# A two-layer graph kernel: all sixteen first-layer tiles split, whole-tile high halves in two buffers, the bias added by an accumulating DMA

## The chip, the cores and the metric

The kernel runs on one core of a Trainium2 chip. The metric is the device time of one execution in microseconds (us). The kernel before takes 984.5 us in the median of three runs.

## The reference

Eight graphs (B = 8) of N = 2048 nodes with F = 128 features. Layer 0 is an attention layer over a dense matrix `adj`, layer 1 a graph convolution with batch normalisation over all eight graphs:

```python
# layer 0, one graph
h = x @ W
e = h @ a1 + (h @ a2).T                 # [N, N]
e = where(e >= 0, e, 0.2 * e)
attention = softmax(adj * e, axis=0)    # over the rows i
x = attention @ h + bias + x
# layer 1, one graph
y = adj @ (x @ W1 + b1)
# over all graphs and nodes
y = relu((y - mean(y)) * rsqrt(var(y) + 1e-5) * gamma + beta)
out = y + x
```

## The kernel before

Everything is held transposed: features (or source nodes j) on the 128 partitions, the 2048 nodes i along the row. A graph is a batch (`bt`, numbered 0 to 7, `par` = its parity) and is worked off in 16 tiles of 128 source nodes, each a 128x2048 block (1 MB) of `adjT`, held in one of 18 slots. Four chunks of 512 columns make up a row; PSUM has four banks `acc0` for layer 0 and four banks `acc1` for layer 1.

Layer 0, one tile t: ScalarE makes the edge scores from the row vector f1 and a column of f2 (`edge`, L533); VectorE multiplies by the adjacency and finds the maximum of each partition (`score`, L656); ScalarE negates it (L540) and takes the exponential with its sum (`exp`, L542); VectorE takes the reciprocal (`recip`, L663); GpSimd scales the 128x128 block of h with it (`scale_h`, L793); TensorE multiplies into `acc0`. In batch 0 and in tiles 0, 4, 8 and 12 of the later batches ("whole" tiles) this is one float32 matmul for each chunk (`layer0`, L406), which the trace shows as two records. In the other twelve tiles of batches 1 to 7 (`SPLIT`) both operands are split into a rounded high half (type fp32r) and a rest: ScalarE writes the high half of the exponentials chunk by chunk into four 2 KB buffers `exp_hi` (`exp_high`, L552), VectorE the rest in place (`exp_low`, L675), GpSimd the halves of hz (L802, L805), and TensorE makes three one-record matmuls for each chunk (`layer0_split`, L420 to L422). `scores` is a ring of four tiles: `edge` of tile t waits until TensorE is done with tile t-4.

Layer 1 of batch b-1 runs on TensorE between the layer-0 tiles of batch b: `layer1` (L441), float32, one tile of it ahead of each layer-0 tile. It is three tiles ahead, so its last one stands ahead of tile 13, and tiles 13, 14 and 15 of layer 0 follow each other directly. `SIGMA` is the order in which layer 1 takes the slots, and so in which they are loaded again.

At the end of a batch come, for each chunk, h of the next batch (`make_h`, L390, out of an x that was loaded to a slot) and the layer-1 input of this batch (`make_support`, L428), which needs `make_xp` on VectorE (L701: attention sum plus residual and bias). ScalarE copies y of the layer just finished from PSUM (L583) and h (L578), VectorE takes statistics of y (L695) and adds b1 (`support_from_psum`, L707). Layer 1 of the batch can start when h is out of `acc1` and the first chunk of the support is ready. GpSimd adds the bias to the residual x (`add_bias`, L811), the bias having been loaded by SyncE into the f1 buffer of that parity, which is free when the last `edge` of the batch is done. There are two f1 buffers.

All transfers are issued by SyncE, in program order: where one waits, all behind it wait. Batch 0 also multiplies the x of all other batches with a1 and a2 (`rows_of_f`, L375). The last layer 1 (batch 7) is split too (L455 to L458).

Of the kernel before, what the change touches and what calls it, by code (L numbers as in the profile page):

```python
# [27 lines left out]
F32 = mybir.dt.float32  # L28
F32R = mybir.dt.float32r
# [5 lines left out]
P = 128  # L35
# [19 lines left out]
def build(nc, adjT, xT, biasT, W, WT, a12, W1, b1, gamma, beta, outT):  # L55
# [8 lines left out]
    ER = 4  # L64

    SPLIT = [t for t in range(NT) if t % 4]

    LAST_SPLIT = list(range(1, NT))
    WHOLE = [t for t in range(NT) if t not in SPLIT]
    NS = NC * len(SPLIT)  # L70


    SIGMA = list(range(PRE, NT - 2)) + [1, NT - 2, NT - 1, 0]
    assert NT % ER == 0 and len(SPLIT) % 2 == 0 and NT - 1 in SPLIT and 0 in WHOLE
# [6 lines left out]
    X_STAGE = {0: slot_of(1, 0), 1: slot_of(1, 1), **{b: NT - B + b for b in range(2, B)}}  # L81
    STAGED = set(X_STAGE[b] for b in range(1, B))

# [4 lines left out]
    with ExitStack() as ctx:  # L88
# [21 lines left out]
        f1_odd, sup_lo = sb_two_types("f1_odd", "sup_lo", [P, N])  # L110
        f1_all = [sb("f1_even", [P, N]), f1_odd]
        region = [sb("region_even", [P, N]), sb("region_odd", [P, N])]
        exp_hi = [sb(f"exp_hi{c}", [P, CH], F32R) for c in range(NC)]
# [17 lines left out]

        wt_sb = scores[ER - 1][:, 0:P]
# [5 lines left out]
        f_sb = f1_all[1][0:NF, :]  # L138
# [7 lines left out]
        bias_loaded = [sem(f"bias_loaded{c}") for c in range(NC)]  # L146
        gb_loaded = sem("gb_loaded")
        f2_loaded = sem("f2_loaded")
        f_stored, f1_loaded = sem("f_stored"), [sem("f1_loaded_even"), sem("f1_loaded_odd")]
        x0_loaded = [sem(f"x0_loaded{c}") for c in range(NC)]  # L150
        x_loaded = [sem(f"x_loaded{c}") for c in range(NC)]
# [6 lines left out]
        whole_used = sem("whole_used")  # L158
        split_used = sem("split_used")
# [16 lines left out]
        ident_set, hz_done, xb_done = sem("ident_set"), sem("hz_done"), sem("xb_done")  # L176
# [7 lines left out]
        def adj_value(bt, t):  # L184

            if t == 0:
                return 16 * (bt.half + 1)
            if t < PRE:
                return 16 * (bt.n + 1)
            return 16 * (bt.n + 1 + (t in STAGED))  # L190

        def chunk_count(bt, t, c):


            return NS * bt.n + NC * SPLIT.index(t) + c + 1

        def wait_l0(eng, bt, t):

            if t in SPLIT:
                eng.wait_ge(split_used, chunk_count(bt, t, NC - 1))  # L200
            else:
                eng.wait_ge(whole_used, len(WHOLE) * bt.n + WHOLE.index(t) + 1)

# [38 lines left out]
        for b in range(2, B):  # L242
            earlier[slot_of(b % 2, 1)] += 1
# [7 lines left out]
        def _(sp):  # L251
# [11 lines left out]

            def load_f1(bt):
                if not (isinstance(bt.n, int) and bt.n < 2):
                    sp.wait_ge(xb_done, NC * (bt.n - 1))
                sp.dma_start(f1_all[bt.par][:, :], f_rows[bt.n - 1].partition_broadcast(P)).then_inc(f1_loaded[bt.par], 16)

            def load_bias(bt):
                sp.wait_ge(edge_out, NT * (bt.n + 1))  # L270
                for c in range(NC):
                    sp.dma_start(f1_all[bt.par][:, cols(c)], biasT[:, cols(c)]).then_inc(bias_loaded[c], 16)
# [6 lines left out]
            def step(bt):  # L279
                nx = bt.next()  # L280
                if is_first(bt):
                    for t in range(1, NT):
                        for b in F_STEP:
                            if max(F_STEP[b], 1) == t:
                                load_x(b, X_STAGE[b])
# [9 lines left out]
                    load_f1(nx)  # L295
                    sp.wait_ge(h_mm, NC)
                    load_adj(nx, 0)
                    for c in range(NC - 1):
                        load_residual(bt, c)
                    load_bias(bt)  # L300
                    load_residual(bt, NC - 1)
                else:
                    pv = bt.prev()
                    for k, t in enumerate(SIGMA):
# [3 lines left out]
                        elif not is_last(bt):  # L308
                            if t == 1:
# [551 lines left out]
```

## Time and profile before

| | us |
|---|---|
| median of three runs (981.13 to 985.25) | 984.5 |
| the profiled execution | 981.78 |
| its span, first to last instruction | 980.0 |
| TensorE busy | 914.9 (93%) |
| ScalarE busy | 802.3 (82%) |
| VectorE busy | 696.0 (71%) |
| GpSimd busy | 439.8 (45%) |

Busy is the time in which an engine has an instruction under way. "Idle before, releaser" is the time an engine stood still ahead of an instruction and what ended it. In a timeline each row has the start, the duration, the engine, the source line, what is written and read, and in square brackets the idle time ahead of it. The records of matmuls overlap a little, so the pitch from one start to the next tells what one costs, not the duration. The granted TensorE clock is 0.986 of full speed over the span.

### The profile page before, as it was taken

How to read it: one execution, taken by the hardware profiler on the slowest of the kernel's cores; microseconds unless marked ns; L12 is line 12 of the kernel's file. 1: busy time of each engine (PE TensorE's matmuls, PEld its weight loads, DVE VectorE, ACT ScalarE, POOL GpSimd, SP SyncE). 2: the span in 40 equal slices, each digit the busy share in tenths (PEclk: the TensorE clock that was granted, in tenths of full speed). 3: DMA queues.
4: the chain of work that ended last, by engine and by line, in shares of the span. 5: the costliest groups of instructions: out<-in, count | busy, mean ns of one | idle time of the engine just before them, and what ended most of it. 6: DMA issues, size and time to landing. Idle time of an engine off the chain costs nothing.

```text
span 980.0 us, 9394 instructions
## 1 busy us (share of the span) xinstructions
PE 914.9 (93%) x3055; PEld 528.9 (54%) x3055; DVE 696.0 (71%) x864; ACT 802.3 (82%) x953; POOL 439.8 (45%) x334
## 2 busy tenths in 40 slices
PE   7998999989999899999999899998999999998970
PEld 4333555555555655556555555556555555555760
DVE  2544477777777867777777967778777777779967
ACT  6877599986999789996999779996999969896746
POOL 1544355562555435562555635553555625554000
PEclk9999999999999999999999999999999999999995
DMA  8956454566456664566456664475546555435968
GB/s 321 422 227 223 158 197 169 215 227 215 176 183 233 212 220 167 214 221 225 172 183 225 225 219 156 168 265 202 204 182 225 190 218 204 168 128 193 385 253 342
DMA packets 45132, 213.91 MB, mean 218 GB/s; under 512 B 5406, under 2 KB 6030, under 8 KB 23438
## 3 DMA queue, kind: packets, MB, share of 16 engines
q1 hardware_dynamic: 45084, 213.32, 59.7%
q8 instruction: 24, 0.39, 0.2%
q14 instruction: 24, 0.20, 0.1%
HBM read 189.07 MB, written 24.23 MB: 218 GB/s over the span
## 4 chain that ended last, share of the span: by engine, by line
PE 79%; DVE 6%; issue 6%; POOL 4%; ACT 3%; DMA 0%; DVEq 0%; SPq 0%; ACTq 0%; POOLq 0%
PE acc L441 40%; PE acc L406 11%; PE acc L421 6%; PE acc L422 6%; PE acc L420 6%; POOL hz L793 3%; PE acc L428 3%; DVE exp_lo L675 3%; PE acc L390 2%; DVE stats L695 2%; PE acc L455 1%; PE acc L457 1%; PE acc L458 1%; ACT scores L542 1%; DVE adj_slot L781 1%
## 5 line engine op out<-in xcount | busy, mean ns | idle before, releaser
L656 DVE CUSTOM_DVE_ANT_0 scores<-scores,adj_slot 128x2048 f32<-128x2048 f32 x128 | 294.0, 2297 | 24.0 <-DMA adj_slot<-adjT 21.4
L675 DVE TENSOR_TENSOR exp_lo<-scores,exp_hi 128x512 fp32r<-128x512 f32 x336 | 268.5, 849 | 35.5 <-ACT exp_hi L552 35.4
L542 ACT ACTIVATE scores<-scores,neg_mx 128x2048 f32<-128x2048 f32 x128 | 256.3, 2002 | 4.2
L793 POOL TENSOR_TENSOR hz<-region_even,rz 128x128 f32<-128x128 f32 x64 | 132.6, 2072 | 222.1 <-DVE rz L663 222.1
L441 PE MATMUL acc<-adj_slot,region_even 128*128 128x512 f32 x512 | 228.8, 592 | 0.0
L552 ACT CAST exp_hi<-scores 128x512 fp32r<-128x512 f32 x336 | 190.6, 615 | 41.0 <-PE acc L422 37.5
L793 POOL TENSOR_TENSOR hz<-region_odd,rz 128x128 f32<-128x128 f32 x64 | 124.2, 1940 | 215.4 <-DVE rz L663 215.4
L420 PE MATMUL acc<-exp_hi,hz_lo 128*128 128x512 f32 x336 | 162.1, 482 | 15.6 <-DVE exp_lo L675 8.7
L441 PE MATMUL acc<-adj_slot,region_odd 128*128 128x512 f32 x392 | 175.2, 592 | 0.0
L406 PE MATMUL acc<-scores,hz 128*128 128x512 f32 x352 | 158.7, 595 | 6.2 <-POOL hz L793 5.0
L441 PEld LDWEIGHTS acc<-adj_slot,region_even 128*128 128x128 f32 x512 | 96.7, 190 | 106.2 <-issue 103.4
L663 DVE RECIPROCAL rz<-zsum 128x1 f32<-128x1 f32 x128 | 20.9, 164 | 184.3 <-ACT scores L542 184.3
L533 ACT ACTIVATE scores<-f_even,f_cols 128x2048 f32<-128x2048 f32 x64 | 127.5, 1993 | 8.2 <-PE acc L406 7.3
L421 PE MATMUL acc<-exp_hi,hz_hi 128*128 128x512 f32 x336 | 131.4, 391 | 0.0
L422 PE MATMUL acc<-exp_lo,hz_hi 128*128 128x512 f32 x336 | 131.2, 390 | 0.0
L533 ACT ACTIVATE scores<-f_odd,f_cols 128x2048 f32<-128x2048 f32 x64 | 127.4, 1993 | 0.5 <-issue 0.5
L441 PEld LDWEIGHTS acc<-adj_slot,region_odd 128*128 128x128 f32 x392 | 74.0, 190 | 81.1 <-issue 79.0
L406 PEld LDWEIGHTS acc<-scores,hz 128*128 128x128 f32 x352 | 65.9, 190 | 94.4 <-issue 93.5
L420 PEld LDWEIGHTS acc<-exp_hi,hz_lo 128*128 128x128 f32 x336 | 63.2, 188 | 53.7 <-issue 21.4
L421 PEld LDWEIGHTS acc<-exp_hi,hz_hi 128*128 128x128 f32 x336 | 63.2, 188 | 26.3 <-issue 16.7
L422 PEld LDWEIGHTS acc<-exp_lo,hz_hi 128*128 128x128 f32 x336 | 63.1, 188 | 13.6
L805 POOL TENSOR_TENSOR hz_lo<-hz,hz_hi 128x128 fp32r<-128x128 f32 x84 | 62.3, 742 | 6.6
(75 smaller groups left out, 676.5 us busy)
## 6 DMA issues: line engine op xcount, KB each, us to landing
adj_slot<-adjT SPq DMA_DIRECT2D x128, 1024.0 KB, 4.8
adj_slot<-xT SPq DMA_DIRECT2D x13, 1024.0 KB, 9.6
adj_slot<-xp_dram SPq DMA_DIRECT2D x8, 1024.0 KB, 6.3
adj_slot<-y_dram SPq DMA_DIRECT2D x7, 1024.0 KB, 6.6
outT<-adj_slot SPq DMA_DIRECT2D x6, 1024.0 KB, 4.7
f_odd<-f_rows SPq DMA_DIRECT2D x4, 1024.0 KB, 6.9
region_even<-xT SPq DMA_DIRECT2D x16, 256.0 KB, 5.5
f_even<-biasT SPq DMA_DIRECT2D x16, 256.0 KB, 6.8
```

Of the source, the lines that this page charges most:

```text
L406: mm = pe.matmul(acc0[c][:, :], hz[e][:, :], scores[e][:, cols(c)], start=(t == 0), stop=(t == NT - 1))
L420: pe.matmul(acc0[c][:, :], hz_lo[e][:, :], exp_hi[c][:, :], start=False, stop=False)
L421: pe.matmul(acc0[c][:, :], hz_hi[m % 2][:, :], exp_hi[c][:, :], start=False, stop=False)
L422: pe.matmul(acc0[c][:, :], hz_hi[m % 2][:, :], exp_lo[e][:, cols(c)], start=False, stop=(t == NT - 1)).then_inc(split_used, 1)
L441: mm = pe.matmul(acc1[c][:, :], region[bt.par][:, tile_cols(t)], slots[slot_of(bt.par, t)][:, cols(c)], start=(k == 0), stop=(k == NT - 1))
L533: act.activation(scores[t % ER][:, :], f1_all[bt.par][:, :], ACT.Prelu, bias=f2_cols[:, bt.n, t:t + 1], alpha=ALPHA).then_inc(edge_out, 1)
L542: act.activation(scores[e][:, :], scores[e][:, :], ACT.Exp, bias=neg_mx[:, e:e + 1], accum_out=zsum[:, e:e + 1]).then_inc(exp_done, 1)
L552: act.copy(exp_hi[c][:, :], scores[e][:, cols(c)]).then_inc(hi_done, 1)
L656: dve.tensor_tensor_reduce(scores[e][:, :], scores[e][:, :], slots[s][:, :], 1.0, NEG_BIG, ALU.mult, ALU.max, mx[:, e:e + 1]).then_inc(max ...
L675: dve.tensor_tensor(exp_lo[e][:, cols(c)], scores[e][:, cols(c)], exp_hi[c][:, :].bitcast(F32), ALU.subtract).then_inc(lo_done, 1)
L793: scaled = pool.tensor_tensor(hz[e][:, :], region[bt.par][:, tile_cols(t)], rz[:, e:e + 1].to_broadcast([P, P]), ALU.mult)
L805: pool.tensor_tensor(hz_lo[e][:, :], hz[e][:, :], hz_hi[m % 2][:, :].bitcast(F32), ALU.subtract).then_inc(hz_done, 1)
```

## The change

All 16 tiles of batches 1 to 7 take the split path. The high halves get two buffers of a whole tile (`hi`, 8 KB a partition each) in place of four chunk buffers: one cast and one subtraction for a tile, except tile 15, which has four parts (`PARTS`). `exp_high` of tile t waits for TensorE's end of tile t-2 (`HR` = 2) and now stands ahead of `edge` of tile t+2. The negation of the maximum goes from ScalarE to VectorE, and the copy of y from PSUM too, where it stands with its statistics ahead of the last `exp_low`. `edge`, `exp` and `exp_high` of the next batch's tile 0 stand ahead of the copies of h; on VectorE, `score` of that tile stands ahead of `make_xp`, and its `exp_low` ahead of `support_from_psum`. There is one f1 buffer, loaded again when all edges of a batch are done. The x for `make_h` is loaded by chunks into the region of the next batch once y has been stored from there. The bias is added to the residual by a DMA from GpSimd's queue that accumulates into SBUF.

```diff
-    SPLIT = [t for t in range(NT) if t % 4]
+    HR = 2
+    PARTS = {t: (NC if t == NT - 1 else 1) for t in range(NT)}
-    SIGMA = list(range(PRE, NT - 2)) + [1, NT - 2, NT - 1, 0]
+    SIGMA = list(range(PRE, NT)) + list(range(PRE))
-        exp_hi = [sb(f"exp_hi{c}", [P, CH], F32R) for c in range(NC)]
+        hi_x, hi = zip(*[sb_two_types(f"hi_x{e}", f"hi{e}", [P, N]) for e in range(HR)])
...
+            def load_x_for_h(bt, c):
+                sp.wait_ge(y_stored[c], 16 * (bt.n - 1))
+                sp.wait_ge(stats_done, NC * (bt.n - 2) + c + 1)
+                sp.dma_start(region[bt.par][:, cols(c)], xT[bt.n][:, cols(c)]).then_inc(xh_loaded[c], 16)
             def load_f1(bt):
-                if not (isinstance(bt.n, int) and bt.n < 2):
-                    sp.wait_ge(xb_done, NC * (bt.n - 1))
+                sp.wait_ge(edge_out, NT * bt.n)
...
                         if k == 14:
                             load_residual(bt, 2)
-                        if k == 14:
-                            load_bias(bt)
-                    load_residual(bt, 3)
+                        if k == 14 and not is_last(bt):
+                            load_f1(nx)
                     for c in range(NC):
                         sp.wait_ge(y_out, NC * pv.n + c + 1)
                         sp.dma_start(y_dram[pv.n][:, cols(c)], region[pv.par][:, cols(c)]).then_inc(y_stored[c], 16)
+                    load_residual(bt, 3)
+                    if not is_last(bt):
+                        for c in range(NC):
+                            load_x_for_h(nx, c)
+                        load_adj(nx, 1)
                 store_xp(bt)
...
             def exp(bt, t):
-                act.wait_ge(max_done, NT * bt.n + t + 1)
-                act.mul(neg_mx[:, e:e + 1], mx[:, e:e + 1], -1.0).then_inc(neg_done, 1)
             def exp_high(bt, t):
-                for c in range(NC):
-                    act.wait_ge(split_used, NS * bt.n + NC * (m - 1) + c + 1)
-                    act.copy(exp_hi[c][:, :], scores[e][:, cols(c)]).then_inc(hi_done, 1)
+                if t >= HR:
+                    wait_l0(act, bt, t - HR)
+                elif bt.n == 1:
+                    act.wait_ge(h_mm, NC * 2)
+                else:
+                    wait_l0(act, bt.prev(), t - HR + NT)
+                for i in range(PARTS[t]):
+                    act.copy(hi[m][:, part_cols(t, i)], scores[e][:, part_cols(t, i)]).then_inc(hi_done, 1)
...
             def add_bias(bt, c):
                 pool.wait_ge(x_loaded[c], 16 * (bt.n + 1))
-                pool.wait_ge(bias_loaded[c], 16 * (bt.n + 1))
-                pool.tensor_tensor(region[bt.par][:, cols(c)], region[bt.par][:, cols(c)],
-                                   f1_all[bt.par][:, cols(c)], ALU.add).then_inc(xb_done, 1)
+                pool.dma_start(region[bt.par][:, cols(c)], biasT[:, cols(c)], accum_op=ALU.add).then_inc(xb_done[c], 16)
```

VectorE's queue at the end of batch 1, before: `exp_lo3` is tile 15, `acc0` into `region_odd` is `make_xp`, `adj_slot0` is the score of the next batch's tile 0.

```order
L663 RECIPROCAL rz<-zsum 128x1 [waits hz_done,exp_done]
L675 TENSOR_TENSOR exp_lo3_70<-scores3,exp_hi0 128x512 [waits hi_done]
...
L695 BN_STATS stats<-region_even 128x6 [waits y_out] x4
L701 TENSOR_TENSOR region_odd<-acc0_0,region_odd 128x512 [waits xb_done,split_used]
...
L701 TENSOR_TENSOR region_odd<-acc0_3,region_odd 128x512 [waits xb_done,split_used]
L656 ISA scores0,mx<-scores0,adj_slot0 128x2048 [waits edge_out,slot_loaded0]
...
L707 TENSOR_TENSOR region_odd<-acc0_0,b1_sb 128x512 [waits xp_stored0,sup_mm]
```

The same place with the change; `acc1` into `region_even` is the copy of y, `exp_lo0` the rest of the next batch's tile 0.

```order
L660 RECIPROCAL rz<-zsum 128x1 [waits hz_done,exp_done]
L692 COPY region_even<-acc1_0 128x512 [waits l1_chunk]
...
L697 BN_STATS stats<-region_even 128x6 [waits y_out] x4
L672 TENSOR_TENSOR exp_lo3_70<-scores3,hi1_73 128x512 [waits hi_done] x4
L651 ISA scores0,mx<-scores0,adj_slot0 128x2048 [waits edge_out,slot_loaded0]
L651 ISA mx 128x1
L654 TENSOR_SCALAR neg_mx<-mx 128x1 [waits max_done]
L703 TENSOR_TENSOR region_odd<-acc0_0,region_odd 128x512 [waits xb_done0,l0_chunk]
...
L703 TENSOR_TENSOR region_odd<-acc0_3,region_odd 128x512 [waits xb_done3,l0_chunk]
L660 RECIPROCAL rz<-zsum 128x1 [waits hz_done,exp_done]
L672 TENSOR_TENSOR exp_lo0_67<-scores0,hi0_72 128x2048 [waits hi_done]
L709 TENSOR_TENSOR region_odd<-acc0_0,b1_sb 128x512 [waits xp_stored0,sup_mm]
```

Copies and statistics of y moved ahead of the last rests, the next score ahead of `make_xp`, and the rest of the next tile 0 between `make_xp` and the support.

ScalarE's queue at the same batch end, before: `scores3` is tile 15, then y, the edge of the next tile 1, and h.

```order
L542 ACTIVATE scores3,zsum<-scores3,neg_mx 128x2048 [waits neg_done]
L552 CAST exp_hi0<-scores3 128x512 [waits split_used,exp_done]
...
L583 COPY region_even<-acc1_0 128x512 [waits l1_chunk]
...
L533 ACTIVATE scores1<-f1_even,f2_cols 128x2048 [waits split_used]
L578 COPY region_even<-acc1_0 128x512 [waits stats_done,y_stored0,h_mm]
```

And with the change; `scores0` and `scores1` are tiles 0 and 1 of the next batch.

```order
L543 ACTIVATE scores3,zsum<-scores3,neg_mx 128x2048 [waits neg_done]
L557 CAST hi1_73<-scores3 128x512 [waits l0_tile,exp_done]
L557 CAST hi1_73<-scores3 128x512 x3
L536 ACTIVATE scores0<-f1_all,f2_cols 128x2048 [waits l0_tile,f1_loaded]
L536 ACTIVATE scores1<-f1_all,f2_cols 128x2048 [waits l0_tile]
L543 ACTIVATE scores0,zsum<-scores0,neg_mx 128x2048 [waits neg_done]
L557 CAST hi0_72<-scores0 128x2048 [waits l0_tile,exp_done]
L580 COPY region_even<-acc1_0 128x512 [waits h_mm]
```

The copies of y have left this queue, and two edges, an exponential and a whole cast now stand ahead of the copies of h.

## Rows read from the trace of the kernel before

**Rows 1.** Stretch of one batch: us, busy time (instructions) of PE, PEld, DVE, ACT, POOL; clock; DMA

```profile
227.30:340.70 113.40, 109.98 (x370) 64.38 (x369) 84.68 (x108) 96.86 (x121) 56.97 (x44) 1.00 0.57 204
```

**Rows 2.** Timeline of PE, batch 3: start, duration, line, operation, records

```profile
401.60 3.60 PE L406 MATMUL acc<-scores,hz 128*128 128x512 f32 x8
405.03 3.60 PE L441 MATMUL acc<-adj_slot,region_even 128*128 128x512 f32 x8
...
411.20 3.59 PE L441 MATMUL acc<-adj_slot,region_even 128*128 128x512 f32 x8
```

**Rows 3.** Timeline of PE at that batch's end and the next one's start

```profile
430.40 3.60 PE L441 MATMUL acc<-adj_slot,region_even 128*128 128x512 f32 x8
...
441.57 0.50 PE L420 MATMUL acc<-exp_hi,hz_lo 128*128 128x512 f32 x1 [0.64 <-POOL hz_lo L805]
...
445.33 1.05 PE L390 MATMUL acc<-w_sb,adj_slot 128*128 128x128 f32 x8
447.40 1.16 PE L428 MATMUL acc<-w_sb,region_odd 128*128 128x128 f32 x8 [1.02 <-DVE region_odd L701]
...
453.76 7.03 PE L441 MATMUL acc<-adj_slot,region_odd 128*128 128x512 f32 x16
```

**Rows 4.** Groups by line: count, total us, mean ns, idle before

```profile
L675 DVE TENSOR_TENSOR exp_lo<-scores,exp_hi 128x512 fp32r<-128x512 f32 x336 | 268.5, 849 | 35.5 <-ACT exp_hi L552 35.4
L542 ACT ACTIVATE scores<-scores,neg_mx 128x2048 f32<-128x2048 f32 x128 | 256.3, 2002 | 4.2
L533 ACT ACTIVATE scores<-f_odd,f_cols 128x2048 f32<-128x2048 f32 x64 | 127.4, 1993 | 0.5 <-issue 0.5
L683 DVE TENSOR_TENSOR adj_lo<-adj_slot,exp_lo 128x2048 fp32r<-128x2048 f32 x15 | 33.8, 2288 | 3.0 <-ACT exp_lo L562 3.0
L562 ACT CAST exp_lo<-adj_slot 128x2048 fp32r<-128x2048 f32 x15 | 28.5, 1917 | 9.2 <-PE acc L458 9.2
```

**Rows 5.** Timeline of DVE at the same batch end

```profile
440.30 4.07 DVE L675 TENSOR_TENSOR exp_lo<-scores,exp_hi 128x512 fp32r<-128x512 f32 x4 [0.48 <-ACT exp_hi L552]
444.30 2.46 DVE L695 BATCH_NORM_STATS2 stats<-region_even 128x6 f32<-128x512 f32 x4
446.68 2.46 DVE L701 TENSOR_TENSOR region_odd<-acc,region_odd 128x512 f32<-128x512 f32 x4
449.06 2.28 DVE L656 CUSTOM_DVE_ANT_0 scores<-scores,adj_slot 128x2048 f32<-128x2048 f32 x1
```

**Rows 6.** Timeline of SP's queue and of POOL: a residual chunk issued, and its bias added

```profile
441.55 0.33 SPq L262 DMA_DIRECT2D region_odd<-xT  x1
...
445.00 1.28 POOL L811 TENSOR_TENSOR region_odd<-region_odd,f_odd 128x512 f32<-128x512 f32 x1 [1.78 <-DMA region_odd<-xT]
```

**Rows 7.** DMA issues: KB of each, median us from issue to landing

```profile
f_odd<-f_rows SPq DMA_DIRECT2D x4, 1024.0 KB, 6.9
region_even<-xT SPq DMA_DIRECT2D x16, 256.0 KB, 5.5
f_even<-biasT SPq DMA_DIRECT2D x16, 256.0 KB, 6.8
...
y_dram<-region_even SPq DMA_DIRECT2D x16, 256.0 KB, 3.8
```

**Rows 8.** Timeline of POOL in batch 0: the scaling of tiles 14 and 15

```profile
97.27 2.50 POOL L793 TENSOR_TENSOR hz<-region_even,rz 128x128 f32<-128x128 f32 x1 [2.39 <-DVE rz L663]
102.16 0.40 POOL L793 TENSOR_TENSOR hz<-region_even,rz 128x128 f32<-128x128 f32 x1 [2.39 <-DVE rz L663]
```

**Rows 9.** Timeline of PE in batch 0 and at its end

```profile
23.04 3.67 PE L406 MATMUL acc<-scores,hz 128*128 128x512 f32 x8 [1.10 <-issue]
28.16 3.67 PE L406 MATMUL acc<-scores,hz 128*128 128x512 f32 x8 [1.45 <-POOL hz L793]
...
78.00 10.93 PE L406 MATMUL acc<-scores,hz 128*128 128x512 f32 x24
...
106.86 1.05 PE L390 MATMUL acc<-w_sb,adj_slot 128*128 128x128 f32 x8
```

More of the change, by code:

```diff
@@ L64, in build @@
     ER = 4
-    SPLIT = [t for t in range(NT) if t % 4]
+    HR = 2
+    PARTS = {t: (NC if t == NT - 1 else 1) for t in range(NT)}
+    NL = sum(PARTS.values())
     LAST_SPLIT = list(range(1, NT))
-    WHOLE = [t for t in range(NT) if t not in SPLIT]
-    NS = NC * len(SPLIT)
-    SIGMA = list(range(PRE, NT - 2)) + [1, NT - 2, NT - 1, 0]
-    assert NT % ER == 0 and len(SPLIT) % 2 == 0 and NT - 1 in SPLIT and 0 in WHOLE
+    SIGMA = list(range(PRE, NT)) + list(range(PRE))
+    assert NT % ER == 0 and NT % HR == 0
     assert F == P and B == 8 and NT == 16 and sorted(SIGMA) == list(range(NT))
@@ L175, in build @@
         hz_scaled = sem("hz_scaled")
-        ident_set, hz_done, xb_done = sem("ident_set"), sem("hz_done"), sem("xb_done")
+        ident_set, hz_done = sem("ident_set"), sem("hz_done")
+        xb_done = [sem(f"xb_done{c}") for c in range(NC)]
         def cols(c):
@@ L587, in step @@
                 for t in range(NT):
-                    exp(bt, t)
+                    if t > 0 or is_first(bt):
+                        exp(bt, t)
                     if t == 0 and is_first(bt):
                         h_from_psum(bt, acc0, [2, 3])
+                    if t > 0 and not is_first(bt):
+                        exp_high(bt, t)
                     if t + 2 < NT:
@@ L713, in step @@
                 for t in range(NT):
-                    if t > 0 or is_first(bt):
-                        score(bt, t)
-                    if t - 1 in SPLIT and not is_first(bt):
-                        exp_low(bt, t - 1)
-                    if t > 0 or is_first(bt):
+                    if t + 1 < NT:
+                        score(bt, t + 1)
+                    if is_first(bt) or t > 0:
                         recip(bt, t)
@@ L722, in step @@
                         f_from_psum()
-                if not is_first(bt):
-                    exp_low(bt, NT - 1)
-                if not is_first(bt):
-                    y_stats(bt.prev())
-                for c in range(NC):
-                    make_xp(bt, c)
+                    if t == NT - 1 and not is_first(bt):
+                        y_from_psum(bt.prev())
+                        y_stats(bt.prev())
+                    if t > 0 and not is_first(bt):
+                        exp_low(bt, t)
                 if not is_last(bt):
@@ L733, in step @@
                 for c in range(NC):
-                    support_from_psum(bt, c)
+                    make_xp(bt, c)
                 if not is_last(bt):
                     recip(nx, 0)
+                    exp_low(nx, 0)
+                for c in range(NC):
+                    support_from_psum(bt, c)
             dve.memset(eps[:, :], BN_EPS).then_inc(eps_set, 1)
@@ L756, in _ @@
             dve.wait_ge(b1_loaded, 16)
+            score(Batch(0, 0, 0), 0)
             steps(dve, step)
@@ L816, in step @@
                     scale_h(bt, t)
-                    if t == NT - 2 and not is_first(bt):
-                        add_bias(bt, 0)
-                        add_bias(bt, 1)
-                for c in range(0 if is_first(bt) else 2, NC):
+                    if t % TC == TC - 1 and t > TC and not is_first(bt):
+                        add_bias(bt, t // TC - 1)
+                for c in range(0 if is_first(bt) else NC - 1, NC):
                     add_bias(bt, c)
```

194 lines of the change are left out of this document (91 added, 103 removed).

## The prediction

> **What bounds the kernel now.** I read the busy times by stage first. A batch in the middle takes 113.3 us, and TensorE has a record under way for 110.0 of them at full granted clock, ScalarE for 96.9, VectorE for 84.7 [rows 1]. The timeline of TensorE then gives the price of a tile by pitch. A whole float32 tile takes 3.43 us (401.60 to 405.03). The layer-1 tile behind it takes the same and ends at 408.46; the next one starts at 411.20, so the split tile between them took 2.74 us [rows 2]. Within a batch nothing stands between these. The stalls are at the batch's end. The last layer-1 tile starts at 430.40 and ends at 433.83; I call that moment zero. Tiles 13 to 15 follow without layer 1 between them: at split pace they would be through at 8.2, in fact they are at 11.5 (445.33). Layer 1 of the batch starts at 19.9 (453.76) [rows 3]. So a batch is 16 x 3.43 of layer 1, 4 x 3.43 and 9 x 2.74 of layer 0 and an end of 19.9: 54.9 + 13.7 + 24.7 + 19.9 = 113.2, the measured pitch. Seven batches have this form, and each microsecond saved in such a chain on TensorE is one of the span, as long as ScalarE, VectorE and GpSimd keep up.
>
> **Term 1, four more split tiles in seven batches.** 28 x (3.43 - 2.74) = -19.3 us, if TensorE stays the bound. ScalarE for a tile: exponential with its read 2.19 (the mean 2.00, the rest by its pitch), edge 1.99, whole cast 1.92 by the cast of the last stage [rows 4]: 6.1, less what overlaps at the seams, against TensorE's 6.17 (3.43 + 2.74). It is close. But the wait is wide: `exp_high` of tile t is released at TensorE's end of tile t-2, and TensorE needs tile t two layer-1 tiles and one split tile later, 3.43 + 2.74 + 3.43 = 9.6 us. Cast 1.9 and rest 2.3 to 3.4 (one instruction of 2.29 in the last stage, four parts of 0.85 now [rows 4]) take 4.2 to 5.3 of them, so a tile can be 4 us late before TensorE notices. `edge` now stands behind that wait; what waits for it is the score of tile t+2, which has the whole next tile's time. VectorE for a tile: score 2.28 [rows 5], rest 2.3 to 3.4, the small ones some 0.4: 5 to 6.1, under 6.17 too. GpSimd splits hz in all tiles, 0.4 a piece when it is free and 2.5 when the score runs beside it [rows 8]; three in a row are inside the same margin. I take the full 19.3.
>
> **Term 2, the batch's end.** I follow the new queues from zero. ScalarE: exponential of tile 15 until 0.8; its cast waits for tile 13's end at 2.7 and is through at 5.2; edges of the next tiles 0 and 1 until 9.1. VectorE: reciprocal at 1.5, then the four copies of y and the statistics, which I price like the statistics' 2.46 each [rows 5], until 6.4; then tile 15's rest in four parts. These take 2.46 without GpSimd beside them and 4.07 with [rows 5]; GpSimd's scaling is over by 4, so 2.5: until 8.9. TensorE follows part by part and ends tile 15 at 9.7, not 11.5. Here the first exchange is lost: `make_support` needs `make_xp`, which now stands behind the score of the next tile: 8.9 + 2.4 = 11.3, `make_xp` until 13.8 [rows 5]. h of chunk 0 needs x, which needs y stored: y out at 2.2, store 3.8, load 3.5 to 5.5 [rows 6, 7]: 9.7 to 11.7, hidden since the first support starts at 12.0 anyway. From there seven blocks of 128-column matmuls take 6.4 (447.40 to 453.76 [rows 3]): through at 18.4. ScalarE: exponential of the next tile 0 from 11.4, cast until 15.5, then h, the last chunk when TensorE has it, 18.1. VectorE: the rest of tile 0 from 15.5 to 17.9, the first chunk of support at 18.6. Layer 1 thus starts at 18.6 to 19.0 (some semaphore hops of 0.1 are in none of these); I take 19.0, for 19.9 before. Six times -0.9, and -0.5 in batch 7, which has no next tile: -6 us.
>
> **Term 3, the bias by DMA.** `add_bias` on GpSimd cost 1.28 to 1.5 a chunk and lay hidden but for the last. Chunks 0 to 2 now go out earlier and are hidden too. Chunk 3: its x is issued behind the four stores of y (four issues of 0.5), at 4.6, lands 3.5 later [rows 6], at 8.1, and only then the accumulating DMA starts. The trace has none. The nearest rows are the same bytes from the same memory: plain loads of 5.5 and 6.8 [rows 7]; its lower bound is the 3.5 of rows 6. Landing is then 11.6 to 14.9. `make_xp` of chunk 3 comes at 13.2 and may be as late as 14.8, since VectorE would next wait for the cast (15.5). So it costs 0 within the bounds. Read from two places, or issued by an engine that is held up, it could take 10: then 3.3 us in each of seven ends, 23 us. That is the widest unknown. I take 0.
>
> The Trainium skill has a rule against this edit (SBUF — State Buffer, section "SBUF: two separate sides", the box on the "DVE blocks DMA" trap): GpSimd writes such a DMA's descriptors itself, and VectorE's two-port operations lock it out meanwhile. The trace shows a lock of that kind for GpSimd's arithmetic: 2.50 us with the score beside it, 0.40 without [rows 8]. By that rule chunk 3 would wait from 8.1 until the score ends at 11.2 and land at 14.7 to 18.0, up to 3.2 us late in an end. The same page infers that operations with two SBUF inputs take only the read side, and then nothing is held up.
>
> **Term 4, batch 0.** VectorE's score of tile t+1 now comes ahead of the reciprocal of tile t, so the scaling doesn't meet it: 0.4, not 2.5 [rows 8]. TensorE's first two idles there, 1.10 and 1.45 [rows 9], shrink by some 2, and behind 78.0 the tiles came every 4.9 us (97.27 to 102.16 [rows 8]) since scaling and score stood in a chain; now TensorE's 3.43 holds: 76 + 7 x 3.43 = 100.0 for 106.9 [rows 9]. But the 7 us do not arrive. The one f1 buffer can be loaded only when the edge of tile 15 is done, at 90 by ScalarE's 4.1 a tile, and takes 6.9 [rows 7]: 97. Edge 99, score 101.4, `make_xp` until 104; the supports end at 108.4 and, since `hi[0]` holds x of batch 1, its cast waits for all of h, 107.6. Cast 109.5, h 111.7, rest 111.9, support 112.6, against 114.0 before. -1.4.
>
> **Sum.** -19.3 - 6 - 1.4 = -26.7 against the profiled execution of 981.8: 955.1. The median of the runs lies 2.7 above that execution, so 957.8; I say 958. The tail behind the last layer 1 is untouched.
>
> **Rivals.** (a) The accumulating DMA is late, 10 us or more from x's landing: its 3.3 to 5 us in seven ends eat the gain, 981 to 993; the sign turns at 10.5 us, and from 11.2 on it is slower by over 0.5%. For it: it is the only transfer that starts so late in a chain, and nothing like it is in the trace. Against: 3 to 7 us is what every transfer of this size takes. Chance 0.12, of it 0.07 slower by over 0.5%. (b) VectorE becomes the bound: if the rests stay at 3.4 (GpSimd beside them in every tile) and GpSimd's three operations lock it for 0.4 to 0.8 each, a tile takes 6.5 or more, +0.35 in some 80 of 112 tiles, 28 us, but 4 us of slack a batch are there first, so it costs 0 to 20: 960 to 978. For it: 84.7 busy already and 16 negations, 4 copies, 4 rests more [rows 1]. Against: whole rests save three seams of four. Chance 0.15. (c) The gain in the tiles is there, but the ends grow, because h waits for x behind y's store (if the loads take 8 each, layer 1 starts at 21 to 22): +2 to 3 in six ends, 970 to 976. Chance 0.13. (d) More than forecast, because the slack behind an end carries further: 948 to 953. Chance 0.08. The forecast, 953 to 966: 0.52.
>
> **The numbers.** The range 950 to 977 leaves out most of (a) and part of (d), about 0.2. A difference under 0.5% (5 us) cannot be told from none here. Faster 0.87 comes of all but (a) and a remainder for what I have overlooked; same 0.05, slower 0.08.
>
> **What would show it.** In the changed profile: split tiles everywhere from the second batch, 2.74 a piece; the batch pitch 109.5 for 113.2; layer 1 starting 19 us after its last tile ended; ScalarE idle for TensorE within a batch; no wait of VectorE for the accumulated chunk 3 over 1 us; batch 1 starting at 112.6. It would be wrong if VectorE's `make_xp` waits for the bias DMA, if TensorE waits for rests inside a batch, or if h waits for x.

## The result, and the profile after

The changed kernel takes 1003.3 us in the median of four runs (1001.5 to 1009.6), beside 983.6 for the kernel before: ratio 1.0214, interval 1.0162 to 1.0265. It is slower by 2.1%, where 958 was forecast. The profiled execution is the slowest of the four, 1009.6.

The page of the changed kernel: span, and busy time of each engine (share, instructions).

```profile
span 1007.8 us, 9249 instructions
PE 917.0 (91%) x3167; PEld 564.2 (56%) x3167; DVE 709.6 (70%) x817; ACT 788.9 (78%) x594; POOL 246.7 (24%) x390
```

No engine became the bound. GpSimd is busy for 44% less, ScalarE 13 us less and VectorE 14 more, and TensorE is as busy as before, although 28 tiles are cheaper: some of it is time at half clock. So the question is where TensorE waits. Seven rows of the list of waits of the changed kernel, those of VectorE on DMAs and of TensorE that bear on it (engine and line, releaser: total us, count, longest):

```profile
DVE scores L651 <- DMA adj_slot<-adjT: 36.9, 7, 7.4
DVE region_odd L703 <- DMA region_odd<-biasT: 20.0, 6, 5.4
DVE region_even L703 <- DMA region_even<-biasT: 18.5, 5, 6.5
PE acc L427 <- POOL hz_lo L810: 13.4, 7, 2.0
PE acc L392 <- DMA region_even<-xT: 9.9, 3, 3.9
PE acc L427 <- DVE exp_lo L672: 7.0, 7, 1.0
PE acc L392 <- DMA region_odd<-xT: 5.2, 3, 2.2
```

`make_xp` (L703) waits 38.5 us for the bias DMA, which was costed at nothing; h (L392) waits 15.1 us for x; and there is a wait inside the batch, seven times 1.9 us for `hz_lo`. The seven waits for a rest (`exp_lo`, 1.0 us each) are those at tile 15's first part, which Term 2 had. So of the three things that the prediction named as its undoing two are there, `make_xp` on the bias DMA and h on x; in place of the third, TensorE waiting for rests inside a batch, it waits for GpSimd. With zero as in the prediction, the ledger of the profiled execution is:

| | forecast | before | after |
|---|---|---|---|
| layer 1 of batch 0 starts at | 112.6 | 114.0 | 116.8 |
| zero to the start of layer 1, six ends | 19.0 | 19.9 to 20.2 | 21.3 to 23.1 |
| the same, last end | 18.4 | 18.9 | 15.1 |
| start of layer 1 to the next zero, seven stretches | 90.5 | 93.3 | 92.8 to 97.3 |

Against the forecast that is 4.2 us in batch 0, 18.9 in the six ends, -3.3 in the last, and 32.6 in the seven stretches between: 52.4 of the 54.5 that this execution missed by (1009.6 to 955.1). The stretches, whose gain the prediction took in full, are the larger part.

**One end.** VectorE at the end that answers to [rows 5], in the changed kernel; zero is 328.85 there:

```profile
334.65 2.48 DVE L672 TENSOR_TENSOR exp_lo<-scores,hi 128x512 fp32r<-128x512 f32 x4
337.05 2.29 DVE L651 CUSTOM_DVE_ANT_0 scores<-scores,adj_slot 128x2048 f32<-128x2048 f32 x1
...
339.45 1.89 DVE L703 TENSOR_TENSOR region_even<-acc,region_even 128x512 f32<-128x512 f32 x3
346.83 0.69 DVE L703 TENSOR_TENSOR region_even<-acc,region_even 128x512 f32<-128x512 f32 x1 [5.50 <-DMA region_even<-biasT]
...
349.70 2.48 DVE L709 TENSOR_TENSOR region_even<-acc,b_sb 128x512 f32<-128x512 f32 x4
...
361.99 2.29 DVE L651 CUSTOM_DVE_ANT_0 scores<-scores,adj_slot 128x2048 f32<-128x2048 f32 x1 [7.42 <-DMA adj_slot<-adjT]
...
364.41 0.17 DVE L660 RECIPROCAL rz<-zsum 128x1 f32<-128x1 f32 x1
```

The rests begin 5.8 us behind zero (forecast 6.4) and end at 8.3 (8.9), and `make_xp` begins at 10.6 (11.3): the queue does what was worked out. Then chunk 3 stands 5.50 us for its bias. GpSimd at the same place, which answers to [rows 6], and behind it:

```profile
337.43 0.89 POOL L815 DMA_DIRECT2D region_even<-biasT  x1 [3.85 <-DMA region_even<-xT]
...
364.65 2.37 POOL L795 TENSOR_TENSOR hz<-region_odd,rz 128x128 f32<-128x128 f32 x1 [13.72 <-DVE rz L660]
366.99 2.44 POOL L807 TENSOR_TENSOR hz_hi<-region_odd,rz 128x128 fp32r<-128x128 f32 x1
369.50 2.46 POOL L810 TENSOR_TENSOR hz_lo<-hz,hz_hi 128x128 fp32r<-128x128 f32 x1
```

x landed 8.6 behind zero (forecast 8.1) and the bias was issued at once. It landed 9.3 us later, 17.9 behind zero, where the limit was 14.8. In the other five of these ends it was issued at 8.7 to 10.3 and took 7.5 to 10.2. The windows show what it met (length, busy time and instructions of PE, PEld, DVE, ACT, POOL; clock, DMA share, GB/s):

```profile
340.00:342.00 2.00, 2.00 (x18) 2.00 (x19) 1.34 (x3) 1.97 (x3) 0.00 (x0) 1.00 1.05 400
352.00:356.00 4.00, 4.00 (x6) 1.61 (x5) 2.54 (x4) 1.39 (x1) 0.00 (x0) 0.50 0.00 0
```

The DMA engines are full for nearly all of the time that the bias is under way (a share of 0.99 from 337 to 347 us). With it go the accumulating DMA of chunk 2 (until 339.7), the four loads of x for h (until 342.7), a tile of adjacency (335.9 to 346.5) and from 340.2 the stores of `xp`; the stores of y had landed at 335.5. TensorE, same kernel:

```profile
347.58 1.16 PE L435 MATMUL acc<-w_sb,region_even 128*128 128x128 f32 x8 [1.13 <-DVE region_even L703]
350.44 10.03 PE L448 MATMUL acc<-adj_slot,region_even 128*128 128x512 f32 x16 [1.70 <-DVE region_even L709]
...
363.06 7.03 PE L448 MATMUL acc<-adj_slot,region_even 128*128 128x512 f32 x16
372.02 0.50 PE L427 MATMUL acc<-hi,hz_lo 128*128 128x512 f32 x1 [1.93 <-POOL hz_lo L810]
```

It stands 1.13 and 1.70 us, starts layer 1 at 21.6 for the 19.9 of [rows 3], and its granted clock falls to 0.50, the 1.2 GHz level, in the second of these waits: two tiles of layer 1 take 10.03 us instead of 7.03. A second loss follows. `recip` of the next batch's tile 1 stands on VectorE behind the score of tile 2, and that score waits 7.42 us for its adjacency, whose load was issued only when the first layer-1 tile freed the slot. So `recip` comes at 364.4, and GpSimd's three operations for tile 1 each fall beside an operation of VectorE: 7.3 us for what takes 1.3 (0.40, 0.40 and 0.46) when it is free. TensorE stands 1.93 us. This is so in all seven batches, in those at full clock too (two stretches of 92.8 at clock 1.00). Of the 32.6 us, 13.4 are these waits, and 16.5 are what the other five stretches have over 92.8, at a mean clock of 0.95 to 0.98; the last 2.7, 0.4 in each stretch, are not assigned.

### The profile page after: what moved, and what is told of

Same layout as the page of the kernel before. It is cut to its first block, busy times and chain, and to the rows that moved or that the text cites. A ratio compares the mean times of both kernels' runs of the same rounds, so it can differ in the third digit from the quotient of the medians.

```text
span 1007.8 us, 9249 instructions
## 1 busy us (share of the span) xinstructions
PE 917.0 (91%) x3167; PEld 564.2 (56%) x3167; DVE 709.6 (70%) x817; ACT 788.9 (78%) x594; POOL 246.7 (24%) x390
## 4 chain that ended last, share of the span: by engine, by line
PE 68%; DMA 12%; DVE 7%; POOL 5%; ACT 3%; issue 3%; DVEq 0%; SPq 0%; ACTq 0%; POOLq 0%
PE acc L448 31%; PE acc L427 8%; PE acc L428 8%; PE acc L429 8%; PE acc L415 3%; DMA adj_slot<-adjT 3%; PE acc L377 2%; DVE scores L651 2%; DMA xp_dram<-region_even 2%; DMA xp_dram<-region_odd 2%; POOL hz_lo L810 2%; POOL hz_hi L807 2%; DMA region_odd<-biasT 2%; POOL hz L795 2%; DMA region_even<-biasT 1%
## 5 line engine op out<-in xcount | busy, mean ns | idle before, releaser
L672 DVE TENSOR_TENSOR exp_lo<-scores,hi 128x2048 fp32r<-128x2048 f32 (+1 forms) x133 | 258.2, 1954 | 133.4 <-ACT hi L557 133.4
L557 ACT CAST hi<-scores 128x2048 fp32r<-128x2048 f32 (+1 forms) x133 | 214.6, 1629 | 74.8 <-PE acc L429 69.8
L536 ACT ACTIVATE scores<-f_all,f_cols 128x2048 f32<-128x2048 f32 x128 | 255.4, 2001 | 17.5 <-PE acc L415 13.3
L427 PE MATMUL acc<-hi,hz_lo 128*128 128x512 f32 x448 | 215.0, 480 | 20.4 <-POOL hz_lo L810 13.4
L428 PE MATMUL acc<-hi,hz_hi 128*128 128x512 f32 x448 | 177.4, 396 | 0.0
L795 POOL TENSOR_TENSOR hz<-region_odd,rz 128x128 f32<-128x128 f32 x64 | 51.1, 798 | 295.7 <-DVE rz L660 286.0
L427 PEld LDWEIGHTS acc<-hi,hz_lo 128*128 128x128 f32 x448 | 85.5, 191 | 65.2 <-issue 31.5
L795 POOL TENSOR_TENSOR hz<-region_even,rz 128x128 f32<-128x128 f32 x64 | 43.4, 678 | 307.8 <-DVE rz L660 307.8
L428 PEld LDWEIGHTS acc<-hi,hz_hi 128*128 128x128 f32 x448 | 85.7, 191 | 36.3 <-issue 21.8
L429 PEld LDWEIGHTS acc<-exp_lo,hz_hi 128*128 128x128 f32 x448 | 85.6, 191 | 18.6
L415 PE MATMUL acc<-scores,hz 128*128 128x512 f32 x128 | 56.9, 598 | 0.0
L415 PEld LDWEIGHTS acc<-scores,hz 128*128 128x128 f32 x128 | 23.7, 190 | 33.1 <-issue 33.1
```

The lines of the kernel that those rows point to most:

```text
L415: l0_done(pe.matmul(acc0[c][:, :], hz[e][:, :], scores[e][:, cols(c)], start=(t == 0), stop=(t == NT - 1)), t, c)
L427: pe.matmul(acc0[c][:, :], hz_lo[e][:, :], hi[m][:, cols(c)], start=(t == 0), stop=False)
L428: pe.matmul(acc0[c][:, :], hz_hi[m][:, :], hi[m][:, cols(c)], start=False, stop=False)
L429: l0_done(pe.matmul(acc0[c][:, :], hz_hi[m][:, :], exp_lo[e][:, cols(c)], start=False, stop=(t == NT - 1)), t, c)
L536: act.activation(scores[t % ER][:, :], f1_all[:, :], ACT.Prelu, bias=f2_cols[:, bt.n, t:t + 1], alpha=ALPHA).then_inc(edge_out, 1)
L557: act.copy(hi[m][:, part_cols(t, i)], scores[e][:, part_cols(t, i)]).then_inc(hi_done, 1)
```

## The experiments

Two theories stood for the main losses: the bias DMA, and the place of `recip`. The rival was that the 1 MB adjacency load of the next tile 1, moved behind the loads of x, is what delays everything. Each ratio is to the kernel before, run again beside the experiment (982.6 to 984.0 us).

**No bias.** The accumulating DMA is gone and `make_xp` waits for x; the bias is left out of the result.

```diff
-                pool.dma_start(region[bt.par][:, cols(c)], biasT[:, cols(c)], accum_op=ALU.add).then_inc(xb_done[c], 16)
-                dve.wait_ge(xb_done[c], 16 * (bt.n + 1))
+                dve.wait_ge(x_loaded[c], 16 * (bt.n + 1))
```

> The changed kernel without its accumulating DMA: the bias of layer 0 is left out of the result, and make_xp waits for the residual's own landing. Theory D (the accumulating DMA of chunk 3 is late and sets the end of each batch): make_xp of chunk 3 no longer waits (5 to 6 us idle of VectorE in most ends in the changed kernel, 38 us in all), layer 1 starts 19 to 20 us after its last tile ended instead of 21.3 to 23.1, and with the clock dips behind these waits the time falls by 20 to 30 us, to 975 to 985. Theory R (VectorE's order is the cause: the score of tile 2 stands ahead of the reciprocal of tile 1 and waits for its adjacency tile): under 10 us, since the 1.9 us gap at tile 1 and the dip behind it stay. Theory X (h waits for x behind y's store): under 8 us.

972.6 us, ratio 0.9900 (0.9872 to 0.9927), 31 less than the changed kernel. The ends are 17.7 to 18.5, but the stretches 92.8 to 96.1: the wait for `hz_lo` is untouched by this.

**`recip` first.** In batches 1 to 7 `recip` of tile 1 stands ahead of the score of tile 2. Nothing is left out.

```diff
                 for t in range(NT):
+                    early = t == 1 and not is_first(bt)
+                    if early:
+                        recip(bt, t)
                     if t + 1 < NT:
                         score(bt, t + 1)
-                    if is_first(bt) or t > 0:
+                    if (is_first(bt) or t > 0) and not early:
                         recip(bt, t)
```

> The changed kernel with one pair exchanged on VectorE in batches 1 to 7: the reciprocal of tile 1 ahead of the score of tile 2. Theory R: the scaling of tile 1 starts 7 to 8 us earlier, beside an idle VectorE, its three operations take 0.4 to 0.5 us each instead of 2.4, TensorE's gap of 1.9 us at tile 1 goes in all seven batches, and so does the half-clock stretch behind it: 15 to 25 us, to 978 to 988. Theory D: the gap goes but the time moves by under 5 us, since the ends of the batches set it.

978.4 us, 0.9961 (0.9945 to 0.9977): one moved instruction is worth 25 us. The scaling of tile 1 by GpSimd in this kernel, and one stretch (columns as above):

```profile
347.90 0.40 POOL L798 TENSOR_TENSOR hz<-region_odd,rz 128x128 f32<-128x128 f32 x1 [6.04 <-DVE rz L660]
348.26 0.40 POOL L810 TENSOR_TENSOR hz_hi<-region_odd,rz 128x128 fp32r<-128x128 f32 x1
348.74 0.46 POOL L813 TENSOR_TENSOR hz_lo<-hz,hz_hi 128x128 fp32r<-128x128 f32 x1
341.37:431.97 90.60, 90.60 (x285) 53.68 (x286) 70.04 (x76) 80.70 (x56) 27.25 (x45) 1.00 0.56 189
```

TensorE is busy for all of 90.60 us. Five of seven stretches are 90.6, the others 92.2 and 93.3. The ends stay at 21.3 to 23.1.

**Adjacency of the next tile 1 early**, issued ahead of the stores of y. Nothing is left out.

```diff
-                        elif t == 0 and not is_last(bt):
+                        elif not is_last(bt):
                             load_adj(nx, t)
...
                             load_x_for_h(nx, c)
-                        load_adj(nx, 1)
```

> The changed kernel with the 1 MB load of the next batch's adjacency tile 1 issued as soon as its slot is free (when layer 1 is done), not behind the four loads of x. Theory C (the late accumulating DMA and the late x loads share the DMA engines with this 1 MB): the bias transfer lands 2 to 3 us earlier (7.0 us median now, 9.4 in the end I read), VectorE's wait for it halves, 8 to 15 us less, 988 to 995. Rival: the accumulating transfer is slow by itself, the 1 MB moves in front of y's store and the x loads instead, and the time stays within 5 us of 1003.

1009.5 us, 1.0276 (1.0237 to 1.0315): a miss. It made it worse. The ends grew to 22.5 to 25.4, h waits 23.7 us for x and VectorE 48.5 for the bias. The bias of chunk 3 did land faster, as that theory had it (6.1 to 7.1 us for 7.5 to 10.2), but x came later, and the bias was issued only 12.1 to 15.0 us behind zero. So ahead of the stores the load is in the way too; it doesn't show that the load is harmless where it was.

**The kernel before with 14 tiles split.** It asks whether the old queues could have had the gain of the tiles. Nothing is left out.

```diff
-    SPLIT = [t for t in range(NT) if t % 4]
+    SPLIT = [t for t in range(NT) if t % 8]
```

> The kernel before with only the list of split tiles changed: 14 split tiles (all but 0 and 8) instead of 12. This is term 1 of the prediction alone, at half size. If TensorE is the bound within a batch and ScalarE's chunk buffers keep up: 2 x 7 x 0.69 = 9.7 us less, 974. Rival: ScalarE at 6.8 us for a split tile against TensorE's 6.17 uses up its lead without the whole tiles 4 and 12 to recover on, TensorE waits for rests near the batch's end, and the gain is 0 to 5 us.

980.6 us, 0.9976 (0.9959 to 0.9993). Each stretch fell by 1.4, as 2 x 0.69 says, but the six ends grew from between 19.9 and 20.2 to between 20.1 and 22.9, and TensorE waits 27.8 us for `hz_lo`. Of 9.7 us, 2.7 arrived.

**Both repairs**: no bias and `recip` first.

> The two edits that each took 25 to 31 us off the changed kernel, together: no accumulating DMA (the bias of layer 0 is left out) and the reciprocal of tile 1 ahead of the score of tile 2. If the late bias and the late reciprocal are two separate losses and explain the whole miss: the stretch from layer 1's start to its last tile's end is 90.5 us in every batch, the end about 18, the time 945 to 955, near the 958 that was forecast. If they hide one another in part (the clock dips belong to either): 955 to 970. If a third loss of that size is left: over 970.

952.3 us, 0.9691 (0.9667 to 0.9715). Six stretches are 90.5 to 90.6 and one 93.2, the ends 17.7 to 18.6. One batch of it from zero to zero (for [rows 1]):

```profile
315.89:424.20 108.31, 106.46 (x386) 67.54 (x384) 86.15 (x100) 95.36 (x72) 28.93 (x48) 1.00 0.57 204
```

The two losses together are 51 us. Singly they are 31 and 25, 5 more in sum. The time at half clock, which belongs to both, accounts for about as much: the stretches exceed the shortest of their kernel by 16.5 us in all in the changed kernel, 11.0 without bias, 4.5 with `recip` first and 3.1 with both. What follows divides the bias DMA's 26 (978.4 to 952.3), always with `recip` first.

**A plain DMA.** `accum_op` is gone, so the bias overwrites the residual x, which is left out of the result.

```diff
-                ... biasT[:, cols(c)], accum_op=ALU.add).then_inc(xb_done[c], 16)
+                ... biasT[:, cols(c)]).then_inc(xb_done[c], 16)
```

> The reciprocal first, and the bias DMA of GpSimd's queue without the accumulation, so that the bias overwrites the residual x (x is left out of layer 0's result): same bytes, same queue, same moment. Base is the reciprocal-first kernel at 978.4. Theory A (adding into SBUF makes the transfer slow): it lands in 3 to 5 us instead of 7 to 9, VectorE's wait for it falls under 10 us in all, 955 to 962. Theory Q (the queue and the traffic beside it make it late): same landing, same 978. Theory of the descriptor lock (VectorE holds GpSimd off): 978 too, with DMA issues on GpSimd longer than 0.9 us.

969.8 us, 0.9872 (0.9847 to 0.9897). The median landing falls from 7.0 to 5.7 us. The accumulation is 9 of the 26; the other 17 stay with a plain transfer from the same queue at the same place.

**The adjacency of the next tile 1 late**, behind the stores of `xp`. Nothing is left out.

```diff
                             load_x_for_h(nx, c)
-                        load_adj(nx, 1)
                 store_xp(bt)
+                if not is_first(bt) and not is_last(bt):
+                    load_adj(nx, 1)
```

> The reciprocal first, and the 1 MB load of the next batch's adjacency tile 1 issued behind the stores of xp, no longer between the x loads and the bias. Theory Q with the traffic as the reason: in the stretch in which the DMA engines are full 1 MB of 3.3 MB is gone, the bias lands about 3 us earlier, 960 to 968; the score of tile 1 may then wait for its tile, but has some 10 us. If the bias is slow by itself (7 us also where nothing else moves): the same 978 or, if the score of tile 1 comes late, 980 to 985.

965.4 us, 0.9817 (0.9798 to 0.9837): half of the 26 comes back with the accumulating DMA unchanged. The DMA issues of the end of batch 2 alone (KB each, median us to landing), first with `recip` first only, then with the load late:

```profile
region_even<-biasT POOLq DMA_DIRECT2D x1, 256.0 KB, 9.2
```

```profile
region_even<-biasT POOLq DMA_DIRECT2D x1, 256.0 KB, 5.5
```

In all six ends it took 7.5 to 9.5 us with the megabyte beside it and 5.5 to 7.7 without: the load is a large part of the lateness of chunk 3. Both this and the plain DMA shorten the same wait; their 13 and 9 aren't parts of a sum.

**Bias out of chunk 3 only**; left out of the result for the last 512 nodes of batches 1 to 7.

```diff
+                if c < NC - 1 or is_first(bt):
                     pool.dma_start(region[bt.par][:, cols(c)], biasT[:, cols(c)], accum_op=ALU.add).then_inc(xb_done[c], 16)
```

> The reciprocal first, and of the four bias DMAs of batches 1 to 7 only the last one left out (the bias is missing in the last 512 nodes). If the whole loss by the accumulating DMAs is chunk 3's place at the end of the chain: the same as without all four, 952 to 955. If the first three cost something too (traffic, GpSimd's 0.9 us issues, the lock): 957 to 970.

962.6 us, 0.9790 (0.9775 to 0.9804). Chunk 3 is 16 of the 26. Chunks 0 to 2, which "are hidden too", cost the other 10: two of the ends are 22.1 and 22.4, where TensorE waits 3.9 and 3.6 us for the x of h. Over all ends these waits are 14.8 us (the two rows), beside 4.7 with no bias DMA at all.

```profile
PE acc L392 <- DMA region_even<-xT: 9.4, 3, 3.9
PE acc L392 <- DMA region_odd<-xT: 5.4, 3, 2.2
```

**The bias added in DRAM**, a batch ahead: x is copied to a scratch tensor at tile 5 and the four accumulating DMAs are issued in a row behind tile 9; the residual is loaded from the scratch. Nothing is left out.

```diff
+                    if t == 5 and not is_last(bt):
+                        pool.dma_start(xb_dram[bt.n + 1], xT[bt.n + 1]).then_inc(xb_copied, 16)
+                    if t == 9 and not is_last(bt):
+                        pool.wait_ge(xb_copied, 16 * (bt.n + 1))
+                        for c in range(NC):
+                            pool.dma_start(xb_dram[bt.n + 1][:, cols(c)], biasT[:, cols(c)], accum_op=ALU.add).then_inc(xb_summed, 16)
```

> A complete kernel: reciprocal first, and for batches 1 to 7 the sum x + bias is made in DRAM one batch ahead (a copy and an accumulating DMA from GpSimd's queue, in the middle of a batch), so that the residual is loaded with its bias and nothing is behind its landing. If the bias's place at the end of a chain is the loss and not the operation: the time of the kernel without the bias, 945 to 960, faster than both kernels by 2 to 3%. Rival: the 4 MB more of DRAM traffic for each batch (copy read and write, two reads and a write of the sum) delay the adjacency loads, 960 to 980.

986.0 us, 1.0043 (1.0018 to 1.0068). The ends are 17.7 to 18.1 as they should be, and all of it is lost again within the batch. GpSimd in this kernel:

```profile
175.05 2.53 POOL L838 DMA_DIRECT2D xb_dram<-biasT  x3
186.66 0.81 POOL L838 DMA_DIRECT2D xb_dram<-biasT  x1 [9.09 <-issue]
```

Three go out in 2.53 us; the fourth stands 9.09 us on the engine, with the scaling of tile 10 behind it, and TensorE waits 27.1 us in all for `hz_lo`.

**The same, spread out.** SyncE copies x; one accumulating DMA is issued behind each of tiles 2, 4, 6 and 8. Nothing is left out.

```diff
+                    if t in (2, 4, 6, 8) and not is_first(bt):
+                        c = t // 2 - 1
+                        if c == 0:
+                            pool.wait_ge(xb_copied, 16 * bt.n)
+                        pool.dma_start(xb_dram[bt.n][:, cols(c)], biasT[:, cols(c)], accum_op=ALU.add).then_inc(xb_summed[c], 16)
```

> A complete kernel, the last one (986.0) mended: x is copied in DRAM by the SyncE queue, and the four accumulating DMAs of a batch are issued from GpSimd one by one behind tiles 2, 4, 6 and 8, not four in a row. There the fourth issue stood 9.1 us for the three before it, and GpSimd's scaling of the next tile came 11 us late. Theory: GpSimd holds at most three such DMAs under way, and it is the fourth issue that cost 33 us against the kernel without a bias (952.3): now 952 to 958. Rival: the DRAM traffic (4 MB a batch more) cost it: 965 to 985.

952.5 us, 0.9686 (0.9672 to 0.9700), the time without any bias. The DRAM traffic of the kernel with four in a row is in this one too, so it was the row and not the traffic that cost. The transfers are not cheap there (5.1 us to landing), but nothing waits for them.

**Batch 0 repaired as well**: there the bias of chunks 0 and 1 goes out behind tiles 13 and 14, and the copies of h and the support stand ahead of cast and rest of the next tile 0. Nothing is left out.

```diff
+                    if t in (13, 14) and is_first(bt):
+                        add_bias(bt, t - 13)
...
-                    exp_high(nx, 0)
+                    if not is_first(bt):
+                        exp_high(nx, 0)
                     h_from_psum(nx, acc1)
+                    if is_first(bt):
+                        exp_high(nx, 0)
```

> The same, and three edits of batch 0 alone: two of its four bias DMAs go out earlier so that no fourth one waits (6 us between the third and the fourth issue before), h is copied from PSUM ahead of the cast of the next tile 0, and the support ahead of its rest. Layer 1 of batch 0 starts at 113.6 in the kernel without a bias, of which 4.1 us is TensorE waiting for the support: I expect 110 to 111, so 3 us less than the run before, 949 to 955. If it is no less, the wait for h (whose copies end at 111.8) is the limit and not the support.

945.5 us, 0.9623 (0.9603 to 0.9644), the fastest of all and ahead of both kernels. Layer 1 of batch 0 starts at 110.65 for 114.20, and the stretch behind it is 90.6 for 93.2. TensorE there, first in the kernel without this repair, then in this one:

```profile
114.20 9.80 PE L461 MATMUL acc<-adj_slot,region_even 128*128 128x512 f32 x16 [4.08 <-DVE region_even L725]
```

```profile
110.65 7.03 PE L461 MATMUL acc<-adj_slot,region_even 128*128 128x512 f32 x16
```

The wait is gone, and with it the half clock behind it: the start is 3.6 us earlier and the stretch 2.7 shorter, most of the 7.0 us that came where only the earlier start, 3, had been counted.

**Three tiles whole again**: that last kernel with tiles 4, 8 and 12 whole in batches 1 to 7. Nothing is left out.

```diff
+    WHOLE = [4, 8, 12]
+    PARTS = {t: (NC if t == NT - 1 else 0 if t in WHOLE else 1) for t in range(NT)}
+    SPLIT = [t for t in range(NT) if t not in WHOLE]
```

> The fastest kernel so far (945.5) with tiles 4, 8 and 12 of batches 1 to 7 whole again: float32, no cast, no rest, no halves of hz. This is term 1 of the prediction by itself, in a kernel whose other losses are mended: 3 x 7 x 0.69 = 14.5 us more, 960, if TensorE is the bound in every batch. Rival: the split of every tile costs a lead of ScalarE and VectorE that whole tiles would give back, then it is under 10 us more, below 956.

961.8 us, 0.9771 (0.9751 to 0.9790): 16.3 more, where 21 tiles at 0.69 are 14.5. The profiled executions tell why: the seven stretches are 14.7 longer in sum, 0.70 a tile (one is 92.60, 225.81 to 318.41, for 90.5), and layer 1 of batch 0 starts at 115.0 for 110.65, where the edit changes nothing; the granted clock was 0.72 there from 12 to 24 us and 0.70 from 100 to 105. Some 3 us come back elsewhere. So the price held, and the excess is not that of the tiles.

## Why the prediction was wrong

**What failed first: Term 3, "I take 0".** In the end read above the chain up to it held to within 0.7 us (x at 8.6 for 8.1; up to 10.3 in others). The size of the landing failed: 9.3 us in that end against a bound of 6.8 from the loads of the kernel before [rows 7]. That bound was a median: the same trace has single loads of the bias of up to 8.9 us, so "3 to 7 us is what every transfer of this size takes" was a wrong reading of its rows. And the place was another one: the DMA share at the batch's end before, from 436 to 446 us, was 0.52, and here, while the bias was under way, 0.99. Median and longest of all 32 are 7.0 and 10.2. Rival (a) had this place and the sign. It priced a landing of 10 us, which came within a microsecond of what this end shows, at 23 us and more; with `recip` first the bias DMAs cost 26. The DMA alone would still have been a small gain: with it and `recip` first the kernel takes 978.4. "Chunks 0 to 2 are hidden too" failed as well, at 10 us: `make_xp` waits little for them (1.5 and 1.4 us in two ends), but with them under way the x of h comes late. The load that was moved there, `load_adj(nx, 1)`, stands in the diff, but its bytes were in no term.

**What failed second: in Term 1, "three in a row are inside the same margin".** Both rows were there, 2.50 and 0.40 [rows 8], and 3 x 2.5 is within 9.6. But the margin was counted from a `recip` that runs when the exponential is ready (356.7 in the end read above). It ran at 364.4, since VectorE is in order and the score ahead of it waited for a slot that only layer 1 frees. Of the 9.6 us this took 7.7, and the three operations, each beside one of VectorE's, 7.3 more. No rival named it. It cost 25 us with the bias DMA in place and 20 without; the waits themselves are 13.4, and the rest goes with the clock behind them.

**What both left out: the clock.** All terms were made at full clock, as the rows of before showed it. In the changed kernel a wait of TensorE at an end costs its own length and, in the end read above, 3 us more in the two tiles behind it; five of the seven stretches show a clock under 1.00.

**What held.** Term 1's price: the stretch is 90.5 at 2.74 a tile, and a whole tile costs 0.70 more, for 0.69. Term 2: without the bias DMA the ends are 17.7 to 18.6 where 19.0 was worked out, and 14.8 in the last for 18.4, a bit pessimistic. Term 4: 112.85 for 112.6 with `recip` first, 113.6 in the kernel with both repairs. With these two losses away the forecast's time is there: 951.8 in the profiled execution against 955.1, and 952.5 in the median with the bias complete. Rivals (b) and (d) fell: no tile waits for VectorE at its rate. Rival (c)'s mechanism, h waiting for x, is real, but through the bias DMAs: without them h waits 4.7 us in three ends together, and all six ends stay under 19.0.

**The rule on "DVE blocks DMA"** did not decide. The rule (the Trainium skill, SBUF — State Buffer, section "SBUF: two separate sides"), as the prediction applied it, would have held the issue of chunk 3 until the score's end. Here it went out at once beside the score, and the 32 issues took 0.88 us in the median. The same page of the Trainium skill infers that an operation with two SBUF inputs leaves descriptor writing alone, and the trace agrees. Its lock for arithmetic agrees too, 2.4 against 0.4 us, and that one did cost time, through the second loss. The landing at 17.9 lies within the 14.7 to 18.0 that the prediction worked out by the rule, but that is luck: nothing held the issue up, and the transfer itself was slow.

**Open.** What share of each loss is the lower clock, since it falls after some ends and not after others with the same idle times (1.13 and 1.70 us in the end above, 1.04 and 1.70 at full clock with `recip` first). The clock was also 0.72 from 12 to 24 us in the profiled executions of four kernels, the changed one among them, and 1.00 in others that run the same instructions there: h of batch 0 took 6.48 us for 3.82. With `recip` first, where batch 0 is the same and this clock is 1.00, layer 1 starts at 112.85 for 116.83, so nearly all of the 4.2 us that the ledger has in batch 0 may be of this.

## What to carry to other kernels

Price a moved transfer at the DMA load of the place it is moved to, with all that the change starts beside it, and ask of every byte whether the chain waits for it or for what it delays; in this kernel the same sum, made a batch ahead and spread out, cost nothing that the times show (952.5 beside 952.3). A margin on an in-order engine begins where the instruction can be reached, not where its input is ready: look at what stands ahead and what that waits for. And a batch end at the limit of its slack deserves a chance of its own in the forecast, since one wait there costs more than its length.

## What the runs showed of the hardware

- **Accumulating DMAs queue on their issuer.** Of four in a row three go out at 0.84 us each and the fourth holds GpSimd. In batch 0 of the changed kernel (into SBUF) it stood 2.43 us and went out 0.3 us behind the first one's landing; in the kernel with four in a row into DRAM it stood 9.09 us and went out 0.3 us behind the landing of all three. No run varied the number or tells what the limit is.
- **An accumulating DMA of 256 KB into SBUF** landed after 4.2, 7.0 and 10.2 us (shortest, median, longest), a plain one from the same queue after 5.7 in the median.
- **Three GpSimd operations in a chain** beside VectorE each waited for one of its operations: 2.37, 2.44 and 2.46 us for 0.40, 0.40 and 0.46.
- **The granted clock** fell to its 1.2 GHz level (0.50) in a 4.08 us wait of TensorE and stayed at 1.00 at the same place when the wait was gone: 9.80 and 7.03 us for the same 16 records.
